# Second cast buffer, weight tiles in halves, kv copy on VectorE, output transposes in psB

## Chip, cores, metric

The kernel runs on all 8 cores of one Trainium2 chip, each with one of the 8 batch rows of `x` ([4096, 2048] float32) and a full copy of the five weight matrices ([2048, 2048] float32). No core talks to another. The metric is the device time of the slowest core in microseconds (us).

## What is computed

A LayerNorm, a causal linear attention with an ELU+1 feature map, and a gate from a projection with ternary weights:

```python
xn = (x - mean) / sqrt(var + 1e-5)
q, k, v = xn @ Wq + bq, xn @ Wk + bk, xn @ Wv + bv      # 16 heads of 128
qf, kf = elu(q) + 1, elu(k) + 1
# chunks of 128 rows; kv_ex, ksum_ex: sums over the chunks before
A = where(causal, qf @ kf.T, 0)
out = (qf @ kv_ex + A @ v) / (qf @ ksum_ex + A.sum(-1) + 1e-6)
s = out @ Wo + bo
scale = mean(abs(W));  Wt = clip(round(W / scale), -1, 1)
y = x + s * silu(layernorm(xn) @ Wt)
```

## The kernel before

The 4096 rows are worked through in 8 superchunks of 512 rows (`for sc in range(nsc)`, L464), each of four chunks of 128 rows. Activations are kept transposed (features on partitions) in bf16: `xnT`, `xn2T` (normalized twice, the input of the ternary projection), `qat`, `kfT`, `vg`, each [128, 16 x 512].

A superchunk is this sequence on TensorE:

- `emit_ln_B` (L421): for each of the four chunks j, 16 transposes of `xns` into the upper half of psB (L431) and 16 of `kftok` or `vtok` (used here for the normalized rows) into the lower half (L437). VectorE copies the lower half to `xnT` (L447), ScalarE scales the upper half to `xn2T` in 16 operations (L455). ScalarE makes the rows of chunks 2 and 3 in `emit_apply` (L409, L414) after the transposes of chunks 0 and 1.
- `proj_phase` (L469) for q, k and v: 16 output tiles each. A tile waits for its weight tile (128 x 2048 bf16, 512 KB) in the ring `wring` and for its bank of psA, and is 16 matmuls of 128 x 512 (L487). ScalarE (L502, L505) and VectorE (L511) take q and k out of psA, ScalarE alone v (L531).
- Attention, four chunks (L540): transposes of kfT and vg into psB (L546, L553), copied to `kftok` by VectorE (L560) and `vtok` by ScalarE (L565); scores into psA (L575), masked to `a_m` (L583, L589); inter plus intra products into psB (L603, L609); the normalizer into psA (L616, L622), its Ln and Exp on ScalarE (L629, L634); the chunk's kv product into psA (L641); VectorE multiplies into `qat` (L649) and adds psA to the float32 state `kvstate` (L657). ScalarE copies the state to bf16 `kvbf` (L669), VectorE adds and copies `ksumst` to `ksumbf` (L663, L666).
- `emit_ln_A` (L330) issues the next superchunk's statistics: VectorE sums (L349), ScalarE squares (L344), a chain of tiny operations, and the applies of chunks 0 and 1 (L389, L394). It is queued ahead of the evacuation of f.
- `proj_phase` for f (evacuated by ScalarE as Silu, L684) and o (L708, L716).
- Output, four chunks (L724): 16 transposes each (L733), VectorE adds them to the residual rows in `xres` (L741), POOL writes `y` (L750) and loads the residual of chunk j+2 (L320) into the same one of two buffers.

The first superchunk also converts the weights. `mk_step_convert` (L196) makes one step per 128 rows of a matrix: SP loads 1 MB into `xres[sl]`, sl = r % 2 (L203); VectorE casts to bf16 into `pcast[sl]` (L219); POOL writes it to the scratch tensor `wsc` in DRAM in two DMAs of 256 KB (L241). For f a first pass takes absolute sums (L209), then after `mk_step_scale` a second pass makes ternary values with three VectorE operations (L223, L226, L230). 16 steps each for q, k, v, o, f sums, one scale step, and 16 ternary steps stand in this order in `pro_steps`. `pump(2)` emits two of them after each chunk of `emit_ln_B` (L461) and after each output tile (L494); `stream_wtile` (L295) first pumps until the matrix it needs is complete. So two conversion steps stand between two weight loads on SP's queue, and two casts behind each tile's evacuation on VectorE's, until tile 8 of the first v phase.

Both entries of `pcast` are the same buffer, and a cast waits for the last write of either kind:

```python
        pcast = [pcast0, pcast0]                       # L142
                for cr in cast_rel:                    # L215
                    if cr is not None:
                        wait("vector", cr[0], cr[1])
```

Each engine runs its own list of instructions in the order in which the Python code emits them; semaphores hold them together. `psA_bank_rel[bk]` is what must have read a bank of psA before TensorE writes it again, `set_rel`/`wait_rel` the same for other buffers.

## Time and profile before

| | us |
|---|---|
| median of 2 runs | 4101.69 (4101.14 to 4102.23) |
| the profiled execution | 4104.62 |
| its span on the slowest core, from the first to the last instruction | 4103.1 |
| spans of the 8 cores | 4083.9 to 4103.1 |
| mean granted TensorE clock of the cores | 0.837 to 0.854 of full |
| TensorE busy with matmuls | 2820.6 (69%) |
| ScalarE busy | 1219.5 (30%) |
| VectorE busy | 973.9 (24%) |
| bytes moved | 581.66 MB, mean 142 GB/s |

The profile is of one execution on the slowest core. An engine's busy time is an average over stages with different limits, so it must be read by stage: the conversion, which lies within the first superchunk, and the seven superchunks after it. "DVE" is VectorE, "ACT" ScalarE, "PE" TensorE, "POOL" GpSimd, "SP" the queue that issues weight loads. "a <- b" in an idle time means that the engine stood before the instruction until b was done.

### The profile page before, as it was taken

The numbers are of one execution on the slowest core, as the hardware profiler recorded it, in microseconds if no ns is written. First come the engines' busy times: TensorE is split into PE (matmuls) and PEld (weight loads), VectorE is DVE, ScalarE is ACT, GpSimd is POOL, SyncE is SP. The second block draws the span as 40 slices with busy tenths as digits, with TensorE's granted clock in tenths as the row PEclk, the third lists the DMA queues.
The fourth block names the chain that finished last, engine by engine and source line by source line (L and its number), as shares of the span: only waits on it lengthen the run. The fifth ranks groups of instructions, "written<-read, shape, count | busy, mean of one in ns | idle before, by whom it ended". The sixth has DMA issues, their size and how long they took to land.

```text
span 4103.1 us, 41611 instructions; the slowest of 8 cores (4083.9 to 4103.1 us)
## 1 busy us (share of the span) xinstructions
PE 2820.6 (69%) x15876; PEld 1457.6 (36%) x15876; DVE 973.9 (24%) x957; ACT 1219.5 (30%) x1712; POOL 196.5 (5%) x268
## 2 busy tenths in 40 slices
PE   1033324346969696969696969786978598769976
PEld 1011111114434443444344434433444344434443
DVE  2111114324112412240223122212132212221221
ACT  4000001005143424342433343334333342424231
POOL 1111110110000000000000000000000000000000
PEclk9966667667989897989798979997998799889988
DMA  5566667452454145414541454235423543243323
GB/s 160 180 196 196 196 193 248 153 171 99 149 189 150 41 144 185 153 45 137 180 153 52 131 183 153 67 118 184 151 82 103 185 144 103 78 169 123 124 74 127
DMA packets 133056, 581.66 MB, mean 142 GB/s; under 512 B 16000, under 2 KB 16096, under 8 KB 108288
## 3 DMA queue, kind: packets, MB, share of 16 engines
q1 hardware_dynamic: 105984, 436.25, 32.8%
q0 software_dynamic: 26880, 142.74, 10.1%
q8 instruction: 134, 2.20, 0.2%
q14 instruction: 58, 0.48, 0.0%
HBM read 503.43 MB, written 75.50 MB: 141 GB/s over the span
## 4 chain that ended last, share of the span: by engine, by line
PE 58%; DMA 16%; ACT 9%; DVE 8%; issue 6%; POOL 2%; DVEq 0%; ACTq 0%; SPq 0%; POOLq 0%
PE psA L487 49%; DMA wsc<-pcast 12%; ACT xn2T L455 3%; DVE pcast L219 2%; POOL wsc L241 2%; ACT scr L629 2%; ACT scr L634 1%; DMA xres<-x 1%; DVE qat L649 1%; PE psB L431 1%; PE psB L546 1%; PE psB L553 1%; DMA y<-xres 1%; DMA wring<-wsc 1%; DVE a_m L583 1%
## 5 line engine op out<-in xcount | busy, mean ns | idle before, releaser
L487 PE MATMUL psA<-xnT,wring 128*128 128x512 bf16 x6144 | 1426.3, 397 | 589.9 <-DMA wring<-wsc 579.1
L487 PEld LDWEIGHTS psA<-xnT,wring 128*128 128x128 bf16 x6144 | 619.8, 101 | 1393.8 <-issue 733.1
L487 PE MATMUL psA<-xn2T,wring 128*128 128x512 bf16 x2048 | 484.0, 402 | 94.6 <-ACT vg L684 49.1
L487 PE MATMUL psA<-qat,wring 128*128 128x512 bf16 x2048 | 443.3, 379 | 0.0
L487 PEld LDWEIGHTS psA<-xn2T,wring 128*128 128x128 bf16 x2048 | 208.9, 103 | 367.1 <-issue 151.3
L487 PEld LDWEIGHTS psA<-qat,wring 128*128 128x128 bf16 x2048 | 200.4, 98 | 241.6
L716 DVE TENSOR_TENSOR xnT<-scr,vg 128x512 bf16<-128x512 f32 x128 | 88.6, 692 | 806.7 <-ACT scr L708 806.7
L502 ACT ACTIVATE scr<-psA,bs_q 128x512 f32<-128x512 f32 x128 | 88.0, 687 | 579.4 <-PE psA L487 572.9
L531 ACT ACTIVATE vg<-psA,bs_v 128x512 bf16<-128x512 f32 x128 | 88.0, 687 | 509.0 <-PE psA L487 509.0
L502 ACT ACTIVATE scr<-psA,bs_k 128x512 f32<-128x512 f32 x128 | 88.0, 687 | 473.6 <-PE psA L487 473.6
L431 PE MATMUL psB<-identb_s,xns 128*128 128x128 bf16 x512 | 59.5, 310 | 234.0 <-ACT xn2T L455 188.8
L708 ACT ACTIVATE scr<-psA,bs_o 128x512 f32<-128x512 f32 x128 | 88.0, 688 | 355.5 <-PE psA L487 355.5
L455 ACT ACTIVATE xn2T<-psB,lnb_sb,lnw_sb 128x128 bf16<-128x128 bf16 x512 | 182.2, 492 | 36.4 <-PE psB L431 36.4
L219 DVE CAST pcast<-xres 128x2048 bf16<-128x2048 f32 x64 | 78.5, 1227 | 476.5 <-DMA wsc<-pcast 476.5
L241 POOL DMA_DIRECT2D wsc<-pcast x160 | 141.1, 886 | 766.6 <-DVE pcast L219 515.1
L511 DVE SCALAR_TENSOR_TENSOR qat<-scr 128x512 bf16<-128x512 f32 x128 | 88.5, 692 | 350.1 <-ACT scr L505 350.1
L511 DVE SCALAR_TENSOR_TENSOR kfT<-scr 128x512 bf16<-128x512 f32 x128 | 88.5, 692 | 342.5 <-ACT scr L505 342.5
L684 ACT ACTIVATE vg<-psA 128x512 bf16<-128x512 f32 x128 | 74.2, 598 | 297.4 <-PE psA L487 297.3
L750 POOL DMA_DIRECT2D y<-xres x32 | 17.2, 537 | 2942.6 <-DVE xres L741 2896.3
L733 PE MATMUL psA<-identb_s,xnT 128*128 128x128 bf16 x512 | 63.7, 253 | 118.3 <-DVE xres L741 110.4
L431 PEld LDWEIGHTS psB<-identb_s,xns 128*128 128x128 bf16 x512 | 52.0, 144 | 240.2 <-issue 240.2
L649 DVE TENSOR_TENSOR qat<-psB,scr 128x2048 bf16<-128x2048 f32 x32 | 73.3, 2292 | 229.3 <-ACT scr L634 229.3
(97 smaller groups left out, 2209.3 us busy)
## 6 DMA issues: line engine op xcount, KB each, us to landing
wring<-wsc SPq DMA_DIRECT2D x640, 512.0 KB, 3.3
wsc<-pcast POOLq DMA_DIRECT2D x160, 256.0 KB, 6.0
xln<-x POOLq DMA_DIRECT2D x32, 1024.0 KB, 10.9
xres<-w_f SPq DMA_DIRECT2D x32, 1024.0 KB, 5.8
xres<-x POOLq DMA_DIRECT2D x32, 1024.0 KB, 7.4
y<-xres POOLq DMA_DIRECT2D x32, 1024.0 KB, 8.1
xres<-w_q SPq DMA_DIRECT2D x16, 1024.0 KB, 5.7
xres<-w_k SPq DMA_DIRECT2D x16, 1024.0 KB, 5.7
```

The lines of the kernel that those rows point to most:

```text
L219: op("vector", lambda e, sl=sl, cs=cslot: e.tensor_copy(cs[:, :], xres[sl][:, :]), [(s_dv, 1)])
L241: return e.dma_start(out=dst.transpose([1, 0, 2]), in_=s2)
L431: op("tensor", lambda e, t=t, xm=xnstm: e.transpose(psBT[:, 2048 + t * 128:2048 + (t + 1) * 128], xm[:, t * 128:(t + 1) * 128], identb[:, ...
L455: op("scalar", lambda e, t=t, j=j: e.activation(xn2T[:, t * T + j * 128: t * T + (j + 1) * 128], psBT[:, 2048 + t * 128:2048 + (t + 1) * 128],
L487: op("tensor", lambda e, k=k, ti=ti, bk=bk, rb=rhs_buf: e.matmul(psA[:, bk * 512:(bk + 1) * 512], wring[k % 6][:, ti * 128:(ti + 1) * 128] ...
L502: op("scalar", lambda e, bk=bk, to=to, esl=esl: e.activation(scr[:, esl[0]:esl[1]], psA[:, bk * 512:(bk + 1) * 512], AF.Exp, bias=biases[b ...
L511: e.scalar_tensor_tensor(dst[:, to * T:(to + 1) * T], scr[:, esl[0]:esl[1]], 1.0, scr[:, rsl[0]:rsl[1]], ALU.min, ALU.add), [(s_dv, 1)])
L531: op("scalar", lambda e, to=to, bk=bk: e.activation(vg[:, to * T:(to + 1) * T], psA[:, bk * 512:(bk + 1) * 512], AF.Identity, bias=biases[ ...
L629: op("scalar", lambda e: e.activation(scr[:, SQ_DUMP[0]:SQ_DUMP[1]], psA[:, :], AF.Ln, bias=epscol_f[:, :]), [(s_ac, 1)])
L649: op("vector", lambda e, j=j: e.tensor_tensor(bass.AP(qat, j * 128, [[NT * T, 128], [T, H], [1, 128]]), psB[:, :].rearrange("p (t c) -> p ...
L708: op("scalar", lambda e, to=to, bk=bk, ssl=ssl: e.activation(scr[:, ssl[0]:ssl[1]], psA[:, bk * 512:(bk + 1) * 512], AF.Identity, bias=bia ...
L716: op("vector", lambda e, to=to, ssl=ssl: e.tensor_tensor(xnT[:, to * T:(to + 1) * T], scr[:, ssl[0]:ssl[1]], vg[:, to * T:(to + 1) * T], A ...
```

## The change

Four parts:

1. `pcast` becomes two buffers, and a cast waits only for the write of the step that used the same one.
2. The weight ring has 10 slots of half a tile (128 x 1024 bf16, 256 KB) where it had 6 of a whole one. `stream_whalf` issues two DMAs per tile; TensorE waits for the first half ahead of the tile and for the second before its ninth matmul, which also gives the first half's slot free.
3. In attention VectorE makes `kvbf` directly (`kvstate` + psA, bf16) before it updates `kvstate`, and `ksumbf` likewise; ScalarE's copy of the state is gone. psA is given free, as before, by the update of `kvstate`. In the next chunk TensorE waits for VectorE's `kvbf`.
4. The output transposes go to the lower half of psB and no longer to banks 0 and 1 of psA; the output add reads psB and gives psB free.

```diff
-        NRING = 6
-        wring = [e_(nc.sbuf_tensor(f"wring{i}", [128, D], CDT)) for i in range(NRING)]
+        NRING = 10
+        wring = [e_(nc.sbuf_tensor(f"wring{i}", [128, D // 2], CDT)) for i in range(NRING)]
...
-        pcast0 = e_(nc.sbuf_tensor("pcast0", [128, D], CDT))
-        pcast = [pcast0, pcast0]
+        pcast = [e_(nc.sbuf_tensor(f"pcast{i}", [128, D], CDT)) for i in range(2)]
...
-                for cr in cast_rel:
-                    if cr is not None:
-                        wait("vector", cr[0], cr[1])
+                cr = cast_rel[sl]
+                if cr is not None:
+                    wait("vector", cr[0], cr[1])
...
-        def stream_wtile(m, to):
+        def stream_whalf(m, to, half):
             k = wtile_ctr[0]
             wtile_ctr[0] += 1
-            if k >= 6:
-                wait("sync", s_wfree, k - 5)
-            if to == 0:
+            if k >= NRING:
+                wait("sync", s_wfree, k - (NRING - 1))
+            if to == 0 and half == 0:
                 pump_until(PRO_READY[m])
                 wait("sync", s_sm[(m, 0)], s_sm[(m, 0)].n)
                 wait("sync", s_sm[(m, 1)], s_sm[(m, 1)].n)
...
-                in_=wsc[MIDX[m], to, :, :, :]), [(s_w[k % 6], 16)])
+                in_=wsc[MIDX[m], to, :, half * 8:(half + 1) * 8, :]),
+               [(s_w[k % NRING], 16)])
...
                 for to in range(NT):
-                    k, wn = stream_wtile(m, to)
+                    kA, wnA = stream_whalf(m, to, 0)
+                    kB, wnB = stream_whalf(m, to, 1)
                     bk = to % 4
-                    wait("tensor", wn[0], wn[1])
...
+                    wait("tensor", wnA[0], wnA[1])
                     for ti in range(NT):
+                        k = kA if ti < 8 else kB
...
+                        if ti == 8:
+                            incs = [(s_wfree, 1)]
+                            wait("tensor", wnB[0], wnB[1])
...
-                wait("vector", s_ac, ac_kvbf)
+                op("vector", lambda e: e.tensor_tensor(
+                    kvbf[:, :], kvstate[:, :], psA[:, :], ALU.add), [(s_dv, 1)])
+                dv_kvbf = s_dv.n
+                wait("vector", s_dv, dv_ksum4)
+                op("vector", lambda e, j=j: e.tensor_tensor(
+                    ksumbf[:, :], ksumst[:, :],
+                    kscur[:, j * H:(j + 1) * H], ALU.add), [(s_dv, 1)])
+                dv_ksbf = s_dv.n
                 op("vector", lambda e: e.tensor_tensor(
                     kvstate[:, :], kvstate[:, :], psA[:, :], ALU.add), [(s_dv, 1)])
                 dv_kvupd = s_dv.n
...
-                op("vector", lambda e: e.tensor_copy(
-                    ksumbf[:, :], ksumst[:, :]), [(s_dv, 1)])
-                wait("scalar", s_dv, dv_kvupd)
-                op("scalar", lambda e: e.copy(kvbf[:, :], kvstate[:, :]),
-                   [(s_ac, 1)])
-                ac_kvbf = s_ac.n
+                dv_kvbf_state[0] = dv_kvbf
...
-                for bk in range(2):
-                    r0 = psA_bank_rel[bk]
-                    if r0 is not None:
-                        wait("tensor", r0[0], r0[1])
+                wait_rel("tensor", "psB")
...
-                        psAT[:, t * 128:(t + 1) * 128],
+                        psBT[:, t * 128:(t + 1) * 128],
...
-                    psAT[:, 0:2048].rearrange("p (t c) -> p t c", c=128),
+                    psBT_lo3d(),
...
-                psA_bank_rel[0] = (s_dv, dv_out)
-                psA_bank_rel[1] = (s_dv, dv_out)
+                set_rel("psB", (s_dv, dv_out))
```

VectorE in the first superchunk, between two attention chunks, before (L649 multiplies into `qat`, L560 is the next chunk's copy of `kftok`; in brackets the semaphores waited for):

```order
L649 TENSOR_TENSOR qat<-psB,scr 128x16x128 [waits pe,ac]
L657 TENSOR_TENSOR kvstate<-kvstate,psA 128x2048 [waits pe,ac]
L663 TENSOR_TENSOR ksumst<-ksumst,kscur 128x16 [waits dv]
L666 CAST ksumbf<-ksumst 128x16 [waits dv]
L560 COPY kftok<-psB 128x2048 [waits pe]
L583 TENSOR_TENSOR a_m<-psA,maskb_s 128x1024 [waits pe]
```

and the same place after (lines of the changed kernel):

```order
L654 TENSOR_TENSOR qat<-psB,scr 128x16x128 [waits pe,ac]
L661 TENSOR_TENSOR kvbf<-kvstate,psA 128x2048 [waits pe]
L665 TENSOR_TENSOR ksumbf<-ksumst,kscur 128x16 [waits dv]
L669 TENSOR_TENSOR kvstate<-kvstate,psA 128x2048
L675 TENSOR_TENSOR ksumst<-ksumst,kscur 128x16 [waits dv]
L565 COPY kftok<-psB 128x2048 [waits dv,pe]
L588 TENSOR_TENSOR a_m<-psA,maskb_s 128x1024 [waits pe]
```

A second addition over 128 x 2048 stands ahead of the update of `kvstate` and of the copy of `kftok`.

VectorE in the first q phase, conversion steps behind a tile's evacuation, before (`st_k0` and `st_k1` are the semaphores of the scratch writes of even and odd steps, `xl0` and `xl1` those of the loads):

```order
L511 SCALAR_TENSOR_TENSOR qat<-scr 128x512 [waits ac]
L219 CAST pcast0<-xres0 128x2048 [waits xl0,st_k0,st_k1]
L219 CAST pcast0<-xres1 128x2048 [waits xl1,st_k0,st_k1]
L511 SCALAR_TENSOR_TENSOR qat<-scr 128x512 [waits ac]
L219 CAST pcast0<-xres0 128x2048 [waits xl0,st_k0,st_k1]
```

and after:

```order
L516 SCALAR_TENSOR_TENSOR qat<-scr 128x512 [waits ac]
L217 CAST pcast0<-xres0 128x2048 [waits xl0,st_v0]
L217 CAST pcast1<-xres1 128x2048 [waits xl1,st_v1]
L516 SCALAR_TENSOR_TENSOR qat<-scr 128x512 [waits ac]
L217 CAST pcast0<-xres0 128x2048 [waits xl0,st_v0]
```

The order is the same; each cast waits for one of the two scratch semaphores.

TensorE at the end of a superchunk, before (L733 the output transposes of all four chunks, L431 and L437 the next LayerNorm's first):

```order
L733 MATMUL psA<-identb_s,xnT 128x128 [waits ac,dv]
L733 MATMUL psA<-identb_s,xnT 128x128 [waits dv] x63
L431 MATMUL psB<-identb_s,xns 128x128 [waits ac,ini,dv]
L431 MATMUL psB<-identb_s,xns 128x128 x15
L437 MATMUL psB<-identb_s,kftok 128x128 x16
```

and after:

```order
L737 MATMUL psB<-identb_s,xnT 128x128 [waits dv,ac]
L737 MATMUL psB<-identb_s,xnT 128x128 [waits dv] x63
L431 MATMUL psB<-identb_s,xns 128x128 [waits ac,ini,dv]
L431 MATMUL psB<-identb_s,xns 128x128 x15
L437 MATMUL psB<-identb_s,kftok 128x128 x16
```

The order is unchanged; both now write psB, and L431's wait for `dv` means the last output add where it meant the last chunk of attention.

## Rows read from the trace of the kernel before

**Rows 1.** The page, part 4: chain that ended last, by line.

```profile
PE psA L487 49%; DMA wsc<-pcast 12%; ACT xn2T L455 3%; DVE pcast L219 2%; POOL wsc L241 2%; ACT scr L629 2%; ACT scr L634 1%; DMA xres<-x 1%; DVE qat L649 1%; PE psB L431 1%; PE psB L546 1%; PE psB L553 1%; DMA y<-xres 1%; DMA wring<-wsc 1%; DVE a_m L583 1%
```

**Rows 2.** Waits: engine, line, waited for: us in total, times, longest.

```profile
PE psA L487 <- DMA wring<-wsc: 579.1, 41, 106.6
...
DVE pcast L219 <- DMA wsc<-pcast: 476.5, 62, 10.4
```

**Rows 3.** Windows by stage: us, PE, PEld, DVE, ACT, POOL, clock, DMA share, GB/s.

```profile
41.00:175.00 134.00, 10.71 (x96) 10.00 (x96) 23.67 (x20) 30.14 (x68) 26.88 (x31) 1.00 0.55 169
190.00:470.00 280.00, 86.64 (x240) 30.18 (x240) 46.43 (x46) 20.04 (x32) 52.86 (x60) 0.64 0.62 196
...
640.00:710.00 70.00, 35.55 (x112) 12.84 (x112) 33.32 (x20) 8.87 (x14) 0.00 (x0) 0.74 0.75 267
726.00:885.00 159.00, 43.78 (x117) 15.01 (x116) 49.67 (x41) 4.81 (x7) 22.91 (x26) 0.59 0.48 152
...
1180.00:1345.00 165.00, 165.00 (x766) 74.83 (x765) 31.02 (x36) 54.89 (x88) 0.00 (x0) 1.00 0.46 153
```

**Rows 4.** The casts of L219 from 190 to 640, and POOL's issues behind one.

```profile
L219 DVE CAST pcast<-xres x48: 1222/1227/1229, 191.8 to 632.6; 128x2048 bf16<-128x2048 f32 x48
...
455.68 1.76 POOL L241 DMA_DIRECT2D wsc<-pcast  x2 [8.42 <-DVE pcast L219]
```

**Rows 5.** Timeline, stage of absolute sums: start, us, engine, line, [idle before].

```profile
674.70 0.67 SPq L304 DMA_DIRECT2D wring<-wsc  x1
...
682.86 5.25 PE L487 MATMUL psA<-xnT,wring 128*128 128x512 bf16 x16 [5.93 <-DMA wring<-wsc]
```

**Rows 6.** Timeline, first casts and last round of the first transposes.

```profile
41.56 1.22 DVE L219 CAST pcast<-xres 128x2048 bf16<-128x2048 f32 x1
...
75.84 1.91 PE L437 MATMUL psB<-identb_s,vtok 128*128 128x128 bf16 x16
...
172.83 1.23 DVE L219 CAST pcast<-xres 128x2048 bf16<-128x2048 f32 x1 [5.25 <-DMA wsc<-pcast]
```

**Rows 7.** Timeline, first and fourteenth ternary step, and TensorE's restart.

```profile
726.37 1.29 DVE L223 TENSOR_SCALAR pcast<-xres,rscale 128x2048 bf16<-128x2048 f32 x1 [0.38 <-DVE rscale L268]
...
883.53 1.29 DVE L223 TENSOR_SCALAR pcast<-xres,rscale 128x2048 bf16<-128x2048 f32 x1 [8.96 <-DMA wsc<-pcast]
...
897.13 26.34 PE L487 MATMUL psA<-xnT,wring 128*128 128x512 bf16 x112 [8.38 <-DMA wring<-wsc]
```

**Rows 8.** Timeline, second superchunk's attention, between two chunks.

```profile
1378.33 2.28 DVE L657 TENSOR_TENSOR kvstate<-kvstate,psA 128x2048 f32<-128x2048 f32 x1
...
1380.97 1.23 DVE L560 COPY kftok<-psB 128x2048 bf16<-128x2048 bf16 x1
1382.25 1.19 PE L575 MATMUL psA<-qat,kfT 128*128 128x128 bf16 x16
...
1383.61 1.23 DVE L583 TENSOR_TENSOR a_m<-psA,maskb_s 128x1024 bf16<-128x1024 f32 x1 [1.42 <-PE psA L575]
```

**Rows 9.** Timeline, after the last chunk: the next LayerNorm and f.

```profile
1414.93 8.87 DVE L349 TENSOR_REDUCE lst<-xln 128x1 f32<-128x2048 f32 x4
...
1424.92 0.16 DVE L359 SCALAR_TENSOR_TENSOR lst<-lst 128x4 f32<-128x4 f32 x1 [0.58 <-ACT scr L344]
...
1438.42 21.87 PE L487 MATMUL psA<-xn2T,wring 128*128 128x512 bf16 x88 [7.02 <-ACT vg L684]
```

**Rows 10.** Timeline, boundary between the second and the third superchunk.

```profile
1559.81 1.86 PE L431 MATMUL psB<-identb_s,xns 128*128 128x128 bf16 x16 [0.21 <-issue]
...
1563.48 2.09 ACT L409 ACTIVATE kftok<-xln,lst 128x2048 bf16<-128x2048 f32 x1 [24.65 <-PE psB L437]
1565.14 2.29 DVE L741 TENSOR_TENSOR xres<-psA,xres 128x2048 f32<-128x2048 bf16 x1 [8.11 <-DMA xres<-x]
```

**Rows 11.** The page, part 6: DMA issues, KB each, us to landing.

```profile
wring<-wsc SPq DMA_DIRECT2D x640, 512.0 KB, 3.3
...
xres<-w_k SPq DMA_DIRECT2D x16, 1024.0 KB, 5.7
```

More of the change, by code:

```diff
@@ L51, in build_nc @@
     prog = {k: [] for k in ("sync", "gpsimd", "scalar", "vector", "tensor")}
-    s_w = [Sem(f"w{i}") for i in range(6)]
+    s_w = [Sem(f"w{i}") for i in range(10)]
     s_xl = [Sem(f"xl{i}") for i in range(2)]
@@ L147, in build_nc @@
         psBT = psB.ap().bitcast(BF16)
-        psAT = psA.ap().bitcast(BF16)
         for s in all_sems:
@@ L303, in stream_wtile @@
                 wait("sync", s_sm[(m, 1)], s_sm[(m, 1)].n)
-            op("sync", lambda e, m=m, to=to, k=k: e.dma_start(
-                out=wring[k % 6][:, :].rearrange("p (t d) -> p t d", d=128),
-                in_=wsc[MIDX[m], to, :, :, :]), [(s_w[k % 6], 16)])
-            return k, (s_w[k % 6], s_w[k % 6].n)
+            op("sync", lambda e, m=m, to=to, k=k, half=half: e.dma_start(
+                out=wring[k % NRING][:, :].rearrange("p (t d) -> p t d", d=128),
+                in_=wsc[MIDX[m], to, :, half * 8:(half + 1) * 8, :]),
+               [(s_w[k % NRING], 16)])
+            return k, (s_w[k % NRING], s_w[k % NRING].n)
         def load_xln(c):
@@ L325, in build_nc @@
         ac_kvbf = 0
+        dv_kvbf_state = [0]
         xres_handover = [False]
@@ L488, in proj_phase @@
                             psA[:, bk * 512:(bk + 1) * 512],
-                            wring[k % 6][:, ti * 128:(ti + 1) * 128],
+                            wring[k % NRING][:, (ti % 8) * 128:(ti % 8 + 1) * 128],
                             rb[:, ti * T:(ti + 1) * T],
@@ L596, in build_nc @@
                 wait("tensor", s_dv, dv_kftok)
-                wait("tensor", s_ac, ac_kvbf)
+                wait("tensor", s_dv, dv_kvbf_state[0])
                 for h in range(H):
@@ L661, in build_nc @@
                     psA_bank_rel[bk] = (s_dv, dv_kvupd)
-                wait("vector", s_dv, dv_ksum4)
+                wait("vector", s_dv, dv_ksbf)
                 vtiny(lambda e, j=j: e.tensor_tensor(
```

## Prediction

> **What bounds the kernel now.** I read the chain of waits first [rows 1]: TensorE's projection matmuls (L487) are 49% of it, and the DMA that writes converted weights to scratch (`wsc<-pcast`) is 12%. Then the list of waits [rows 2]: VectorE stood 476.5 us in front of the weight cast for that DMA, and TensorE 579.1 us for weight tiles (`wring<-wsc`). The windows by stage [rows 3] (columns: window, length, PE, PEld, DVE, ACT, POOL busy, granted clock, DMA share, GB/s) put all of it in the first superchunk: from 190 to 470 us PE is busy 31% of the time at a mean clock of 0.64 of full, while in the steady q, k and v phases (1180 to 1345) it is busy without a gap at clock 1.00, with the DMA engines at a share of 0.46. So there are two kernels: a conversion stage to about 897 us, bound by one chain (cast, write to scratch, next cast), and seven superchunks of about 420 us (from L431 at 1559.8 [rows 10] there are six of them, and the output's tail, to the end at 4103.1), bound by TensorE with stalls at attention, at the start of f and between superchunks. The change takes the chain of the first apart, and adds to the stalls of the second.
>
> **Conversion: two cast buffers.** A cast now waits for the write of the step before it; after, for that of the step two before.
>
> q, k and v weights of the later steps and o: 48 casts start from 191.8 to 632.6 us [rows 4], so one step takes (632.6 - 191.8)/47 = 9.38 us: cast 1.2, the handover and two POOL issues of 0.88 each (1.76 for two), the landing. With two buffers that whole cycle covers two steps, so 4.7 us a step is the floor of this loop. The next limit is the DMA engines. Two steps and one weight tile are 18.76 us and carry 196 GB/s x 18.76 = 3.68 MB; at the share of 0.62 that is 11.6 us of engine time, 5.8 us a step. In the stage of absolute sums (640 to 710) the engines carry 267 GB/s at 0.75, or 356 at a full share: 10.3 us, 5.2 a step. A third loop goes over two tiles: qat/kfT on DVE, two casts, the weight load, 16 matmuls, ACT. Its load took 8.2 us behind two 1 MB loads (issue at 674.70, PE at 682.86) [rows 5], then PE 5.3, ACT an estimated 1.5, DVE 3: 18 us per four steps, not binding. Bounds per step are thus 5.2 (nothing but bandwidth) and 9.4 (no gain). I take 6.0, a little above the engine time at 0.62, since landings lengthen as the queues fill: 47 x (9.38 - 6.0) = 159 us less, all on the path, since TensorE waits for it.
>
> The first 16 casts: from 41.6 to 172.8 us, 8.75 us each. The first eight are interleaved with the first LayerNorm's four rounds of transposes and copies, which ACT paces; the last round ends at 77.8 [rows 6], so the eighth cast comes at about 78. The last eight carry no weight tile: engine time 0.55 x 8.75 = 4.8 us a step (the window from 41) [rows 3], and I take 5.2, 42 us in all: the last at 120 and not 172.8, 53 us less.
>
> Ternary steps: DVE does 3.8 us each (three operations), from 726.4 to 883.5 thirteen steps at 12.1 us [rows 7]; the tile that closes the stall (PE at 897.13) is queued on SP behind the load that waits for this one. Two buffers allow 6.05 a step, the engine time 0.48 x 24.2/2 = 5.8. I take 6.5: 13 x 5.6 = 73 us less. Bounds 6.05 to 12.1.
>
> Absolute sums write nothing to scratch and keep their 20.5 us per two tiles: 0, perhaps 1 us less per tile, since PE starts on half a tile.
>
> Sum of the first stage: 53 + 159 + 73 = 285 us less (with all low bounds 330, with 8.0 a step throughout about 160).
>
> **The kv state (attention).** Before, DVE adds psA into kvstate at 1378.33 (2.28 us), which frees psA; ACT makes the bf16 copy beside it; DVE copies kftok at 1380.97; the scores (L575) start at 1382.25, held by PE's own transposes, and the mask follows at 1383.61, 1.36 later [rows 8]. After, DVE does the bf16 sum into kvbf first, then ksumbf, and only then the kvstate add that frees psA: 1378.33 + 2.2 + 0.17 + 2.28 = 1382.98, plus 0.25 of semaphore: L575 at 1383.2, about 1.0 us late. kftok is ready by then (1380.97 + 2.2 + 1.23 = 1384.4, just before the mask at 1384.6). The new op is not in the trace; its nearest row is the same add into f32, 2.28 us. If bf16 output ran twice as fast the delay would be 0; the other end is 2.4 (all of it in series). I take 1.0, three times per superchunk, 24 in all: 24 us. The copy taken from ACT (1.9 us) gives nothing here: what the next matmuls wait for is the mask, not ACT's vtok.
>
> After the last chunk f's first tiles start 2.4 us later but then stop anyway for ACT, which is in the next LayerNorm [rows 9]: PE resumes at 1438.42. In that LayerNorm DVE's four sums (8.87 us from 1414.93) begin 2.3 us later and ACT's squares 0.7 later, so the variance (L359, 1424.92, held by ACT) becomes DVE's and comes 1.8 later. Seven times 1.8, and once 2.4 at the end: 15 us. Here ACT's freed 1.9 us stops counting, since DVE is late next.
>
> **Output transposes into psB.** Before, they share psA banks 0 and 1 with nobody who waits. After, they share psB with the next LayerNorm's transposes (L431), which wait for both its parts. In [rows 10] L431 starts at 1559.81, beside the wait for the last residual load; the last output add runs 1565.14 to 1567.43, and after an add PE starts some 0.3 us later (in rows 8 the mask follows its matmuls as closely). After, L431 waits until 1567.7: 7.9 us. Behind it queue L437, ACT's applies (1563.48), ACT's 16 scalings and the whole ACT-bound stage up to q's first matmul, so nothing absorbs it. The other boundaries have the same two loads in front; I take 7.8 x 7 = 55 us. The gain is nothing: the first output transposes never waited for a psA bank, and q's banks are free long before q starts. This term is the surest.
>
> **Weight halves.** Twice the DMAs, five tiles of room instead of six, and a wait amid each 16 matmuls. In the steady phases PE never waits for weights; 766 matmuls in 165 us are 3.45 us per tile of 16 [rows 3], against 3.41 for 16 x 512 columns at 2.4 GHz, so all that a tile boundary with its waits now costs is 0.04 us: 0 taken for another wait, at most 0.04 x 640 = 26 us. The Trainium skill (DMA: Bandwidth & Descriptors, Measured) speaks against this part: batch transfers to 1 MiB, since each pays a fixed part. By it 512 KB take about 3.2 us, and the trace has that (3.3 from issue to landing [rows 11]); halves would take about 2.6.
>
> Sum: -285 + 24 + 15 + 55 = -191. Against the profiled execution's 4104.6 that is 3913.6; the median of the runs shown, 4101.7, is 2.9 lower: 3911, which I round to 3910, 4.7% less.
>
> **The rivals.**
> 1. VectorE's casts block POOL's issues. Until now no cast could run while POOL issued a write to scratch, since each waited for the writes; with two buffers they meet. If each cast held POOL, or was held, for its full 1.23 us, a step would cost 7.2, not 6.0: 47 x 1.2 + 13 x 1.2 + 8 x 1.2 = 82 us back, 3992. For it: the casts' speed (2048 elements in 1.23 us, against 2.28 for an f32 add). Against: POOL is busy only 1.8 of 6 us a step. The Trainium skill (SBUF — State Buffer, the shared port pair) says that a cast in a 2-port mode locks GpSimd out of the port with which it writes descriptors. The trace of before has no overlap to test it. Chance 0.12.
> 2. The DMA side gives out sooner: 8 cores at once, landings that grow with the load, 8.0 us a step. Then the gains are 47 x 1.38 = 65, 13 x 4.1 = 53 and, with 6.9 a step in the first part, 40: 158 less, 94 more, 4038. Against: 267 GB/s at 640 to 710, in the same stage on all cores. Chance 0.07.
> 3. Slower: the landing of the scratch writes stretches in proportion, so that two in flight take as long as one after the other. Its place is `wsc<-pcast`, its price the whole 285 us, and the 94 us of steady additions stand: 4196, 2.3% slower. It decides from a step of 9.0 us on, where 47 x 0.4 + 13 x 3.1 + 35 is the 94 again. Against: the write's engine time is small beside its landing, and 0.38 of the engines' time is free [rows 3]. Chance 0.03. Another one on this side: if two halves don't overlap and each needs over 1.73 us of the steady 3.45 per tile, PE stalls; at a whole tile's 3.3 us each, by 3.1 us a tile, far slower. Against: in the stage at 640 to 710 several transfers of one queue are clearly in flight. Chance 0.02.
> 4. The change isn't effective in conversion because another wait stands right behind (the weight load into `xres`, still two buffers). It lands in 5.7 us [rows 11] against 12 us of cycle per buffer, so it stays inside the 6.0 a step of the forecast.
>
> **How the numbers follow.** The forecast's mechanism has 0.76; 0.12, 0.07 and 0.05 as above. Its own range: all low bounds (-330, and 15 less of attention) 3850; 6.8 us a step 3965. With rival 1 inside, and a little beyond the low bound, the range is 3845 to 3995. Faster by over 2% (below 4020, about what a measurement here can tell from no change): 0.76 + 0.12, less 0.01; within 2% 0.08; slower 0.05.
>
> **What would show it.** Right: casts about 6 us apart between 140 and 420, the DMA share there over 0.9, the wait of casts for `wsc` down from 476 to under 300 us; q's first matmul near 130, the free run of v before 620 (897 now); superchunks 420 + 7.8 + 4.7 = about 432 us long; L431's wait for the last output add, 7.8 x 7; `L575` waiting about 0.8 for DVE; no PE wait for `wring` after the first superchunk. Wrong: POOL's issue longer than 0.89 us (rival 1), casts near 8 us apart (rival 2), superchunks of 420 (the psB term false), or any `wring` wait in q, k, v of the later ones.

## The result, and the profile after

The changed kernel takes 4009.5 us (median; the lowest run is 3991.3), the kernel before 4102.4 beside it on the same chip: a ratio of 0.977, with a 95% interval from 0.974 to 0.980. In some executions of every kernel here the cores of one die, or of both, show a lower granted clock and take longer; the medians are of all executions, the ratios of the others alone. It is faster by 2.3%, about 95 us, where 191 were forecast; 3910 was predicted, and the time lies above the range's end of 3995. The profiled execution took 3996.1 us with a span of 3994.5 on core 1; the spans of the eight cores run from 3961.7 to 3994.5. All positions of these two kernels below are of core 1, as before; each experiment is read on its own slowest core, where no other is named.

The page after, part 4, the chain that ended last by line (against [rows 1]):

```profile
PE psA L492 50%; DMA wsc<-pcast 6%; ACT xn2T L455 3%; DMA y<-xres 3%; DMA wring<-wsc 2%; DVE kvbf L661 2%; ACT scr L634 2%; ACT scr L639 2%; DMA xres<-x 1%; PE psB L431 1%; PE psB L608 1%; DVE lst L349 1%; PE psB L614 1%; POOL wsc L239 1%; PE psA L580 1%
```

The scratch writes fell from 12% of the chain to 6%. New in it are `kvbf` (L661) and three lines of attention on TensorE (L580, L608, L614). The list of waits after (engine, line, waited for: us in total, times, longest), against [rows 2]:

```profile
PE psA L492 <- DMA wring<-wsc: 337.9, 46, 65.9
...
ACT scr L634 <- PE psA L627: 218.3, 32, 8.1
...
DVE pcast L217 <- DMA wsc<-pcast: 152.2, 45, 10.1
...
PE psB L431 <- DVE xres L745: 56.9, 7, 8.9
...
PE psA L580 <- DVE ksumst L675: 21.7, 24, 1.0
```

TensorE's wait for weight tiles is 241 us shorter, VectorE's for the scratch writes 324 us. The last two are the forecast's new waits, of about the forecast size. (The profile names `ksumst` L675 in the last row; by the code L580 waits for the update of `kvstate`, L669, just before it.) The second row is not in the forecast at all: ScalarE waits 218.3 us for the last matmuls of attention's denominators, which in the kernel before was 149.2 (ACT L629 for PE L622, 32 times). TensorE hands over 69 us later in all, and its own wait for VectorE is only 21.7 of that.

The windows by stage (columns as in [rows 3]): the conversion in q, k and v, the ternary steps, a steady stretch of matmuls, one attention chunk.

```profile
125.00:450.00 325.00, 144.16 (x402) 50.09 (x403) 83.04 (x76) 31.72 (x50) 97.51 (x100) 0.70 0.91 288
...
541.00:630.00 89.00, 33.46 (x97) 11.78 (x96) 49.45 (x39) 4.83 (x7) 31.09 (x27) 0.71 0.78 260
950.00:1115.00 165.00, 163.98 (x760) 74.39 (x761) 31.78 (x37) 55.70 (x90) 0.00 (x0) 1.00 0.53 150
1151.00:1172.00 21.00, 12.21 (x128) 11.44 (x128) 10.90 (x9) 5.75 (x3) 0.00 (x0) 0.66 0.00 1
```

The conversion's DMA share rose from 0.62 to 0.91 and its rate from 196 to 288 GB/s. TensorE's steady stretch is as it was; the DMA share there is 0.53 for 0.46 at about the same rate, which costs nothing in it. The attention chunk's window has the same 128 matmuls as that of a chunk before, but in 21 us and not 17, and at a mean granted clock of 0.66. The same window of the kernel before:

```profile
1378.00:1395.00 17.00, 9.50 (x128) 8.92 (x128) 8.33 (x8) 7.64 (x4) 0.00 (x0) 0.80 0.00 1
```

### The conversion stage

The casts of L217 in q, k and v (against [rows 4]), and all issues of L239:

```profile
L217 DVE CAST pcast<-xres x48: 1219/1227/1680, 147.4 to 436.2; 128x2048 bf16<-128x2048 f32 x48
...
L239 POOL DMA_DIRECT2D wsc<-pcast x160: 885/885/1831, 41.7 to 644.8; - x160
```

(436.2 - 147.4)/47 = 6.14 us a step, forecast 6.0. The step was right; what was lost lies at the ends. The sixteenth cast comes at 129.4 instead of 172.8, 43 us earlier (forecast 53): the eighth comes at 80.1, nearly where the forecast had it, and the eight steps behind it take 6.2 us each and not 5.2. From the last of the 48 casts (before at 632.6) to the first ternary step the absolute sums take 99.7 instead of 93.8 us: 6 more (forecast 0); why is not shown. The thirteen ternary steps run from 535.9 to 625.0, 89 us for 157 (forecast 73 less, measured 68). And then something new, TensorE's restart and the first attention:

```profile
645.66 2.15 POOL L311 DMA_DIRECT2D xln<-x  x4
```

```profile
657.16 1.89 PE L492 MATMUL psA<-xnT,wring 128*128 128x512 bf16 x8 [1.45 <-DMA wring<-wsc]
662.03 2.30 PE L492 MATMUL psA<-xnT,wring 128*128 128x512 bf16 x7 [2.98 <-DMA wring<-wsc]
```

As soon as POOL has issued the last scratch write it issues six loads of 1 MB of the next inputs (four for `xln`, two for `xres`), and beside these 6 MB TensorE stops for single halves, five times. From the fourteenth ternary step to the first attention it takes 65 instead of 53 us, 11 more. The six loads alone don't do that. The kernel with two cast buffers and whole tiles (e1, below) issues them as well, and its last 112 matmuls run in one piece:

```profile
655.39 24.33 PE L486 MATMUL psA<-xnT,wring 128*128 128x512 bf16 x112 [2.98 <-DMA wring<-wsc]
```

Over the eight cores the stretch from the fourteenth ternary step to the first attention takes 52 to 56 us in e1 (mean 53.5), 52 to 68 in the changed kernel (60.2) and 53 to 67 in e4, which has the halves and is otherwise e1 (61.0). In sum attention begins 247 us earlier on this core (936.9 to 689.5); forecast 285.

### The steady stage

Attention, VectorE's and TensorE's rows between two chunks (against [rows 8]):

```profile
1149.85 2.29 DVE L654 TENSOR_TENSOR qat<-psB,scr 128x2048 bf16<-128x2048 f32 x1 [8.55 <-ACT scr L639]
1152.06 2.28 DVE L661 TENSOR_TENSOR kvbf<-kvstate,psA 128x2048 bf16<-128x2048 f32 x1
...
1154.34 2.28 DVE L669 TENSOR_TENSOR kvstate<-kvstate,psA 128x2048 f32<-128x2048 f32 x1
...
1159.13 1.23 DVE L588 TENSOR_TENSOR a_m<-psA,maskb_s 128x1024 bf16<-128x1024 f32 x1 [0.95 <-PE psA L580]
...
1170.39 2.29 DVE L654 TENSOR_TENSOR qat<-psB,scr 128x2048 bf16<-128x2048 f32 x1 [8.90 <-ACT scr L639]
```

```profile
1157.09 1.86 PE L580 MATMUL psA<-qat,kfT 128*128 128x128 bf16 x16 [0.90 <-DVE ksumst L675]
...
1160.56 0.31 PE L614 MATMUL psB<-a_m,vtok 128*128 128x128 bf16 x1
1160.66 0.31 PE L608 MATMUL psB<-qat,kvbf 128*128 128x128 bf16 x1
...
1164.61 0.26 PE L627 MATMUL psA<-a_m,onescol_b 128*128 128x128 bf16 x1
1164.71 0.22 PE L621 MATMUL psA<-qat,ksumbf 128*128 128x128 bf16 x1
1164.77 0.22 PE L627 MATMUL psA<-a_m,onescol_b 128*128 128x128 bf16 x1
```

The same place on TensorE in the kernel before (L575, in [rows 8], stands behind L553):

```profile
1378.89 1.87 PE L546 MATMUL psB<-identb_s,kfT 128*128 128x128 bf16 x16 [3.67 <-DVE qat L649]
1380.55 1.91 PE L553 MATMUL psB<-identb_s,vg 128*128 128x128 bf16 x16
...
1385.04 0.22 PE L609 MATMUL psB<-a_m,vtok 128*128 128x128 bf16 x1
1385.09 0.22 PE L603 MATMUL psB<-qat,kvbf 128*128 128x128 bf16 x1
```

L580 begins 1.1 us later behind L661 than L575 did behind L657 (5.03 for 3.92), as forecast. But its 16 matmuls take 1.86 instead of 1.19 us, and then the matmuls of L608 and L614 start 0.107 us apart, until 1164.61; from there on 0.055 apart. All of them started 0.055 apart in the kernel before. The two distances are the lower and the upper level of TensorE's clock (1.2 and 2.4 GHz). Before, the engine went without a gap through its two rounds of transposes (L546, L553, at the lower level) into L575, and the clock rose there. After, it stands for 0.90 us in front of L580, and the clock rises only 7.5 us after L580's start. From 1160.56 to 1164.61 there are 38 distances at 0.107 instead of 0.055: 2.0 us. The chunk takes 20.54 us, for 17.00 (L649 at 1376.12 and 1393.12): 1.1 of waiting, 0.7 in L580, and 1.7 from the mask to the last denominator.

Over the eight superchunks of this core the three distances between L654s add up to 481.0 us, for 412.3 before: 68.7 more, 2.9 a chunk. Forecast 24.

Not every chunk has this form. In 23 of these 24, between 29 and 40 of the 64 matmuls from L608 to L627 run at the lower level (none of them in the kernel before). But in seven of the 24 L580 itself is at the upper level, in spite of its stand, and in six of those the clock falls again behind it:

```profile
1137.72 1.05 PE L580 MATMUL psA<-qat,kfT 128*128 128x128 bf16 x16 [0.99 <-DVE ksumst L675]
...
1140.76 0.27 PE L608 MATMUL psB<-qat,kvbf 128*128 128x128 bf16 x1
```

From 1140.76 the matmuls start 0.107 us apart, until 1144.13.

The next LayerNorm (against [rows 9]) and a boundary between superchunks (against [rows 10]):

```profile
1193.11 2.28 DVE L661 TENSOR_TENSOR kvbf<-kvstate,psA 128x2048 bf16<-128x2048 f32 x1
...
1207.50 0.16 DVE L359 SCALAR_TENSOR_TENSOR lst<-lst 128x4 f32<-128x4 f32 x1 [0.17 <-DVE lst L356]
...
1221.41 3.15 PE L492 MATMUL psA<-xn2T,wring 128*128 128x512 bf16 x7 [7.34 <-ACT vg L691]
```

```profile
1347.91 2.29 DVE L745 TENSOR_TENSOR xres<-psB,xres 128x2048 f32<-128x2048 bf16 x1 [7.28 <-DMA xres<-x]
...
1350.35 1.86 PE L431 MATMUL psB<-identb_s,xns 128*128 128x128 bf16 x16 [7.25 <-DVE xres L745]
```

The variance (L359) now follows VectorE's own sums and not ScalarE, and TensorE resumes f 28.3 us after L661 where it was 26.1 after L657: 2.2 a superchunk (forecast 1.8). L431 waits 7.25 us here for the last output add, 56.9 in all over seven boundaries, 8.1 each (forecast 7.8).

So on core 1: 247 less, then 69 in attention, 18 in LayerNorm and f, 57 at the boundaries more; that gives -103, and the spans differ by 4103.1 - 3994.5 = 108.6. The two gaps against the forecast are 38 us at conversion and 45 us at attention.

### The profile page after: what moved, and what is told of

It is laid out like the page before. It is cut to its first block, busy times and chain, and to the rows that moved or that the text cites. A ratio compares the mean times of both kernels' runs of the same rounds, so it can differ in the third digit from the quotient of the medians.

```text
span 3994.5 us, 43386 instructions; the slowest of 8 cores (3961.7 to 3994.5 us)
## 1 busy us (share of the span) xinstructions
PE 2860.2 (72%) x15876; PEld 1499.8 (38%) x15876; DVE 1049.1 (26%) x989; ACT 1161.7 (29%) x1680; POOL 218.7 (5%) x268
## 4 chain that ended last, share of the span: by engine, by line
PE 58%; DMA 14%; ACT 9%; DVE 8%; issue 8%; POOL 1%; DVEq 0%; SPq 0%; ACTq 0%; POOLq 0%
PE psA L492 50%; DMA wsc<-pcast 6%; ACT xn2T L455 3%; DMA y<-xres 3%; DMA wring<-wsc 2%; DVE kvbf L661 2%; ACT scr L634 2%; ACT scr L639 2%; DMA xres<-x 1%; PE psB L431 1%; PE psB L608 1%; DVE lst L349 1%; PE psB L614 1%; POOL wsc L239 1%; PE psA L580 1%
## 5 line engine op out<-in xcount | busy, mean ns | idle before, releaser
L431 PE MATMUL psB<-identb_s,xns 128*128 128x128 bf16 x512 | 59.6, 309 | 285.2 <-ACT xn2T L455 193.1
L239 POOL DMA_DIRECT2D wsc<-pcast x160 | 163.2, 1024 | 474.4 <-DVE pcast L217 264.3
L431 PEld LDWEIGHTS psB<-identb_s,xns 128*128 128x128 bf16 x512 | 52.0, 142 | 291.6 <-issue 291.6
L737 PE MATMUL psB<-identb_s,xnT 128*128 128x128 bf16 x512 | 63.9, 253 | 118.5 <-DVE xres L745 110.4
L565 DVE COPY kftok<-psB 128x2048 bf16<-128x2048 bf16 x32 | 39.2, 1225 | 364.5 <-PE psB L551 358.4
```

The costliest lines, as they stand in the source:

```text
L239: return e.dma_start(out=dst.transpose([1, 0, 2]), in_=s2)
L431: op("tensor", lambda e, t=t, xm=xnstm: e.transpose(psBT[:, 2048 + t * 128:2048 + (t + 1) * 128], xm[:, t * 128:(t + 1) * 128], identb[:, ...
```

## The experiments

Ratios are to the kernel before, run on the same chip; the interval is at 95%. Three edits recur: the kv part and the psB part (output transposes) taken back to the kernel before, word for word, and the second cast buffer alone.

**One part at a time.** e1 is the kernel before with two cast buffers, and five whole weight slots where it had six, so that they fit:

```diff
-        NRING = 6
+        NRING = 5
...
-        pcast0 = e_(nc.sbuf_tensor("pcast0", [128, D], CDT))
-        pcast = [pcast0, pcast0]
+        pcast = [e_(nc.sbuf_tensor(f"pcast{i}", [128, D], CDT)) for i in range(2)]
...
-                for cr in cast_rel:
-                    if cr is not None:
-                        wait("vector", cr[0], cr[1])
+                cr = cast_rel[sl]
+                if cr is not None:
+                    wait("vector", cr[0], cr[1])
```

> The kernel before with the second cast buffer alone (the ring has 5 whole tiles instead of 6, for room). Theory: the conversion gain is all this part's, TensorE restarts in v about 250 us earlier (near 645, before 897), and the superchunks keep their 419.6 us: about 4100 - 250 = 3850 us. Rival, the halves feed TensorE sooner in the conversion: whole tiles cost 5 us per tile pair there, the gain is some 50 us smaller, 3900.

Measured: 0.943 (0.936 to 0.950), 3870.5 in the profiled execution. The 48 casts stand from 149.0 to 445.9, 6.3 us a step.

e2 is the changed kernel with the kv part taken back:

```diff
-                op("vector", lambda e: e.tensor_tensor(
-                    kvbf[:, :], kvstate[:, :], psA[:, :], ALU.add), [(s_dv, 1)])
...
+                wait("scalar", s_dv, dv_kvupd)
+                op("scalar", lambda e: e.copy(kvbf[:, :], kvstate[:, :]),
+                   [(s_ac, 1)])
```

> The changed kernel without the kv part. Theory (the clock of TensorE rises later because its scores matmuls wait 0.9 us for psA): attention chunks 1 to 3 go from 20.4 back to 17.0 us and f resumes 2.2 us sooner: 24 x 3.4 + 7 x 2.2 = 97 us less, 3900. Rival (only the 1.0 us of the longer VectorE chain, the rest has another cause): 24 + 15 = 39 us less, 3958.

Measured: 0.957 (0.955 to 0.959), against 0.977 for the changed kernel: the kv part costs 0.020, 82 us, nearer to the theory's 97 than to the rival's 39; the two intervals (0.002 and 0.003 either way) leave the 39 out. L608 and L614 are back at the upper level in every chunk (x512 each, over the whole run):

```profile
L614 PE MATMUL psB<-a_m,vtok 128*128 128x128 bf16 x512 | 63.8, 219 | 0.0
L608 PE MATMUL psB<-qat,kvbf 128*128 128x128 bf16 x512 | 63.8, 219 | 52.5 <-DVE a_m L588 50.6
```

The same groups in the changed kernel (busy us, mean ns):

```profile
L614 PE MATMUL psB<-a_m,vtok 128*128 128x128 bf16 x512 | 97.5, 284 | 0.0
L608 PE MATMUL psB<-qat,kvbf 128*128 128x128 bf16 x512 | 96.5, 282 | 50.2 <-DVE a_m L588 49.8
```

e3 takes back the psB part instead:

```diff
-                wait_rel("tensor", "psB")
+                for bk in range(2):
+                    r0 = psA_bank_rel[bk]
+                    if r0 is not None:
+                        wait("tensor", r0[0], r0[1])
...
-                        psBT[:, t * 128:(t + 1) * 128],
+                        psAT[:, t * 128:(t + 1) * 128],
```

> The changed kernel with the output transposes in psA again. Theory: L431 no longer waits for the last output add (8.1 us, 7 times): 57 us less, 3940. Rival, the time comes back in a wait for the residual loads or for ScalarE: 0 to 20 us less, 3980.

Measured: 0.962 (0.960 to 0.964): the psB part costs 0.015, 62 us (forecast 55), and the wait of the first LayerNorm transposes for `xres` is gone from the list.

e4 takes back both, so that what is left is e1 with half tiles for whole ones:

> The changed kernel with both kv and psB undone, so second cast buffer and weight halves. Theory: the parts add up, 97 + 57 less: 3843, and within 10 us of the cast buffer alone (halves worth nothing either way). Rival: halves cost in the conversion (more transfers on a full DMA): 20 us or more above the cast buffer alone; or they gain there, 20 or more below.

Measured: 0.946 (0.940 to 0.952). Beside e1's 0.943 the two intervals overlap nearly whole, so the ratio shows neither a gain nor a cost of the weight halves; one of 30 us would not show in it. The traces say a little more. In e4 the first attention comes at 701 us, in e1 at 687 (means of the eight cores). The stretch behind the fourteenth ternary step, above, has 7.5 us of that; the rest is no more than what kernels with the same conversion differ by (688 in the changed kernel, 700 in e2). From there to the end the eight cores need 3170 us in e4 and 3162 in e1 (means), and on the slowest core of each it is 3174.6 and 3175.8. In the steady stretch a tile costs what it did (760 matmuls in 165 us above). So the halves gained nothing and, in these traces, cost some 7 us at the restart. This answers to the rule weighed in the prediction, the Trainium skill's advice to batch transfers (DMA: Bandwidth & Descriptors, Measured): a half landed in 2.8 us (page after, part 6) where a whole tile took 3.3, so the fixed part is there to see, but it is hidden where TensorE has 3.45 us of work per tile. Only in the stretch after the ternary steps do stops for single halves show; the slowest core of e1 has two stops there, that of e4 five.

**Is it the stand of TensorE?** If a stand of under 1 us in front of the scores is what costs the clock, the kernel before must show the same with such a stand and nothing else. e5 puts a VectorE addition of 1600 columns (its result is not used) between the kvstate update and the copy of `kftok`, in the first three chunks, and lets the scores wait for it:

```diff
+                if j < NCH - 1:
+                    op("vector", lambda e: e.tensor_tensor(
+                        scr[:, 0:1600], kvstate[:, 0:1600], kvstate[:, 0:1600], ALU.add),
+                       [(s_dv, 1)])
+                    for bk in range(4):
+                        psA_bank_rel[bk] = (s_dv, s_dv.n)
```

> The kernel before, with one more VectorE operation (an add of 1600 columns into scratch space that nobody reads, 1.8 us) between ksumbf and kftok for chunks 0 to 2, which psA's release waits for: TensorE stands about 0.8 us before the scores matmuls, as in the changed kernel, but all its other work is as before. Theory (a stand of TensorE there delays the rise of its clock): the chunk takes 17.0 + 0.8 + 2.3 = 20.1 us, with the 64 matmuls of L603 to L622 at 0.11 us instead of 0.055 each for more than half of them; 24 x 3.1 = 74 us above before. Rival (no such effect, the changed kernel's extra comes from the bf16 sum itself or its buffers): 17.8 us, 24 x 0.8 = 19 us above.

Measured: 1.013 (1.010 to 1.015), 52 us: between the theory's 74 and the rival's 19. One chunk of e5, first VectorE, then TensorE:

```profile
1382.67 1.82 DVE L669 TENSOR_TENSOR scr<-kvstate 128x1600 f32<-128x1600 f32 x1
...
1386.98 1.22 DVE L583 TENSOR_TENSOR a_m<-psA,maskb_s 128x1024 bf16<-128x1024 f32 x1 [1.36 <-PE psA L575]
```

```profile
1384.95 1.86 PE L575 MATMUL psA<-qat,kfT 128*128 128x128 bf16 x16 [0.71 <-DVE scr L669]
1388.35 0.27 PE L603 MATMUL psB<-qat,kvbf 128*128 128x128 bf16 x1 [1.54 <-DVE a_m L583]
1388.41 0.31 PE L609 MATMUL psB<-a_m,vtok 128*128 128x128 bf16 x1
1388.52 0.31 PE L603 MATMUL psB<-qat,kvbf 128*128 128x128 bf16 x1
```

It is the changed kernel's picture: 0.71 us of standing, L575 in 1.86, then distances of 0.107. The chunk takes 20.25 us. The three distances of all superchunks add up to 467.2, for 412.3 before: 54.9 more, of which 24 x 0.71 = 17 is standing and the rest is clock. 18 of the 24 chunks have 30 to 43 of their 64 matmuls (L603 to L622) at the lower level and take 19.1 to 20.9 us; the other six have none and take 17.8 to 18.3, which is the standing alone. The second adds and ScalarE's copy, which differ between the kernels, are not needed for the effect.

e6 is the same with 1150 columns, a stand of some 0.3 us:

> The same with 1150 columns (1.35 us): TensorE stands 0.3 us. Theory, if any stand at all delays the clock: 17.3 + 2.3 = 19.6 us a chunk, 62 us above before. If the delay grows with the stand: about 18.2. Rival without a clock effect: 17.3, 7 us above.

Measured: 1.004 (1.001 to 1.008). Most chunks take 17.3 to 17.6 us, but four of 24 take 18.7 to 19.0, with L603 at a mean of 228 ns (269 in e5, 219 before). The shorter stand costs the clock less often: chunks with matmuls from L603 to L622 at the lower level are 0 of 24 without a stand, 4 behind one of some 0.3 us, 18 behind some 0.71, and 23 behind some 0.90 in the changed kernel. Each count is from one execution of one core.

e7 goes the other way. It is the changed kernel, where TensorE repeats eight of its transposes of `vg` in chunks 1 to 3 while it would stand:

```diff
+                for h in range(8 if j > 0 else 0):
+                    op("tensor", lambda e, h=h, j=j: e.transpose(
+                        psBT[:, 2048 + h * 128:2048 + (h + 1) * 128],
+                        vg[:, h * T + j * 128: h * T + (j + 1) * 128],
+                        identb[:, :]))
```

> The changed kernel with 8 repeated transposes ahead of those of vg in chunks 1 to 3, which write what the real ones write again: TensorE is busy in the 0.9 us in which it stood before the scores matmuls. They start no sooner. Theory: the clock rises before L608, the chunk falls from 20.4 to about 18.1 us, 24 x 2.3 = 55 us less than the changed kernel. Rival (the stand isn't the cause): 20.4 us or more, no gain.

Measured: 0.965 (0.962 to 0.969), 47 us faster than the changed kernel for doing more work (the two intervals leave some 19 us either way). In the chunk below the stand shrinks to 0.45 us, and L585 and all behind it are at the upper level:

```profile
1142.68 1.05 PE L585 MATMUL psA<-qat,kfT 128*128 128x128 bf16 x16 [0.45 <-DVE ksumst L680]
1145.28 0.22 PE L613 MATMUL psB<-qat,kvbf 128*128 128x128 bf16 x1 [1.55 <-DVE a_m L593]
```

The distances between chunks add up to 446.1, 35 less than in the changed kernel. The scores start no sooner, so that the 1.1 us of waiting stays in every chunk (26 of the 69 us); the 35 are most of the other 42. 17.97 us is the best chunk, and eight of 24 still have half of their short matmuls at the lower level and take 19.3 to 19.5. The eight transposes both fill the stand and give the engine work ahead of it; which of the two holds the clock is not told apart.

**Can the kv part be had without the stand?** e8 and e11 update kvstate first, which frees psA as early as before, and then copy it to bf16 on VectorE, SBUF to SBUF:

```diff
-                op("vector", lambda e: e.tensor_tensor(
-                    kvbf[:, :], kvstate[:, :], psA[:, :], ALU.add), [(s_dv, 1)])
-                dv_kvbf = s_dv.n
...
+                op("vector", lambda e: e.tensor_copy(
+                    kvbf[:, :], kvstate[:, :]), [(s_dv, 1)])
+                dv_kvbf_state[0] = s_dv.n
```

> The changed kernel with the kv part in another order on VectorE: kvstate is updated first and psA given free, then kvbf is copied from kvstate in SBUF (about 1.2 us), nothing on ScalarE. Theory: psA is free as early as before, TensorE doesn't stand before the scores, kftok comes 1.2 us later but still before the mask: 17.0 to 17.4 us a chunk, 75 us less than the changed kernel. Rival (any second pass on VectorE costs its own length): 18.2 us, 50 less.

e8 gave no ratio. The same kernel was run again, as e11:

> The same kernel as e8, whose comparison didn't come to a verdict. Its undisturbed cores had all 64 matmuls at 0.055 us each and chunks of 17.2 us. Theory: 24 x 3.3 us less than the changed kernel (0.9768 of before, about 4007), so 3925 to 3935, a ratio of 0.957 to 0.960, like the kernel without the kv part (0.9568). Rival, something else on VectorE grows by the extra pass: 0.965 or more.

Measured: 0.964 (0.953 to 0.974), its lowest run 3921.9. The interval is wide and takes in both theories, 0.957 to 0.960 and 0.965 or more; the trace decides. The chunk shown takes 17.27 us, and the copy costs 1.23 in place of a second add of 2.28:

```profile
1128.02 2.29 DVE L654 TENSOR_TENSOR qat<-psB,scr 128x2048 bf16<-128x2048 f32 x1 [7.16 <-ACT scr L639]
...
1132.78 1.23 DVE L675 CAST kvbf<-kvstate 128x2048 bf16<-128x2048 f32 x1
...
1145.29 2.29 DVE L654 TENSOR_TENSOR qat<-psB,scr 128x2048 bf16<-128x2048 f32 x1 [7.16 <-ACT scr L639]
```

L608 and L614 are at 219 ns on average again. Nothing stands in front of the scores, and the clock stays. Over all 24 distances the chunks take 411.1 us, for 412.3 in the kernel before: made in this order, the copy on VectorE has no price in attention that can be seen.

**What bounds a conversion step at 6.1?** e9 is e1 with the loads of the q, k, v and o weights halved; the second half of their columns is stale, so the kernel leaves out half of that input traffic and the output is not the reference's.

```diff
+                nc_ = 1024 if (mode == "cast" and not (m == "q" and r < 2)) else 2048
...
-                    out=xres[sl][:, :], in_=w_in[m][r * 128:(r + 1) * 128, :]),
+                    out=xres[sl][:, 0:nc_], in_=w_in[m][r * 128:(r + 1) * 128, 0:nc_]),
```

> The cast-buffer kernel (e1) with the conversion loads of q, k, v and o cut to half their columns (0.5 MB for 1 MB), so that wrong weights are made from the second half; casts and scratch writes keep their size. It tells what bounds a step, 6.4 us in the changed kernel. Theory, the DMA engines (share 0.91): 3.68 MB per two steps become 2.63 MB, a step falls to about 4.8 us, the floor of the scratch-write loop being 4.7. Rival, the scratch-write loop itself, stretched by POOL and VectorE blocking each other: 6.0 us or more a step.

One execution: 3816.6 us, casts from 139.6 to 405.0, 5.65 us a step. It fell between the two expectations. The windows of e9 and of e1 over the same stretch:

```profile
125.00:440.00 315.00, 150.34 (x437) 53.08 (x438) 90.55 (x81) 34.17 (x54) 97.99 (x97) 0.73 0.76 232
```

```profile
125.00:440.00 315.00, 136.96 (x384) 47.94 (x384) 75.84 (x72) 30.39 (x48) 91.08 (x98) 0.68 0.90 282
```

At a share of 0.76 a step of 5.65 us holds 4.3 us of engine time, so the engines alone don't set it. The step lost 0.7 of 6.3, and the scratch write still took 7.3 us to land (8.2 in e1). An estimate from these rows: cast 1.2, two issues 2.0 and the landing 7.3 are 10.5 us of the 11.3 that a buffer's two steps take in e9, and 1.2, 1.9 and 8.2 are 11.3 of 12.6 in e1. The step is thus mostly the write's own loop, and the load on the DMA engines comes in through the landing, 6.0 us in the kernel before. The forecast's floor of 4.7 for this loop kept the landing as it was. One execution bears this, and how much of the landing is load is not settled.

e10 is e1 with the casts on ScalarE, where they take 1.90 us, to see what VectorE's casts do to POOL:

```diff
-                    op("vector", lambda e, sl=sl, cs=cslot: e.tensor_copy(
-                        cs[:, :], xres[sl][:, :]), [(s_dv, 1)])
...
+                    op("scalar", lambda e, sl=sl, cs=cslot: e.copy(
+                        cs[:, :], xres[sl][:, :]), [(s_ac, 1)])
```

> The cast-buffer kernel (e1) with the casts of q, k, v and o on ScalarE (about 2.0 us each) instead of VectorE (1.2 us, in which POOL can't issue). Theory (VectorE's casts hold up POOL's issues): all 128 issues behind them take 0.89 us again, none 1.4 or 1.8; the step hardly moves, since the DMA engines bound it: 6.2 to 6.6 us, the whole within 10 us of e1. Rival (the blocking is what keeps a step above 6.0): 20 us or more below e1. Rival without any blocking by VectorE: the long issues stay.

Measured: 0.941 (0.937 to 0.945), beside e1's 0.943 (0.936 to 0.950): no difference. POOL's issues from 125 to 440, first of e10, then of e1 (busy us, mean ns):

```profile
L247 POOL DMA_DIRECT2D wsc<-pcast x100 | 88.3, 887 | 229.0 <-ACT pcast L223 211.1 <-issue 17.8
```

```profile
L240 POOL DMA_DIRECT2D wsc<-pcast x98 | 92.0, 943 | 228.3 <-DVE pcast L218 201.4 <-issue 26.3
```

So VectorE's casts do hold up POOL: 943 ns for an issue, and 887 without them. But the step stays at 6.1 us. The casts on ScalarE are 0.67 us longer than on VectorE, and stand in the same loop, so a gain of that size from the shorter issues could be hidden.

e1 and e10 beat both kernels: 3866 and 3854 in their lowest runs, 5.7 and 5.9% less than before.

## Why the prediction was wrong

Its direction and most of its mechanisms held; the gain was half of what it said. By its steps:

- **Step of 6.0 us in q, k and v: right.** 6.14, at a share of 0.91 as foretold, and 152 us less for 159.
- **The ends of the conversion: mis-sized.** "53 us less" for the first casts was 43 (its step of 5.2 was 6.2), "73" for the ternary steps 68, the absolute sums took 6 more for 0, and the restart of TensorE 11 more for 0. The last had no term: the prediction did not ask what POOL issues right behind the last scratch write, and how half tiles fare beside it. What lengthened the first casts and the absolute sums stays open. 247 less on core 1, not 285; over the eight cores the first attention comes on average 243 us earlier.
- **Attention: the step that failed.** "I take 1.0, three times per superchunk, 24 in all: 24 us." The 1.0 us was right for the start of the scores (1.1), and its cost was 2.9 us a chunk, 69 in all. The delay was taken as a delay of VectorE's chain, with no term for TensorE's clock. It is also a stand of TensorE ahead of 80 short matmuls, and in 23 of 24 chunks the granted clock then was at its lower level for about half of them: e5 makes 2.3 us a chunk in the kernel before by a stand of 0.71 alone, e7 takes 35 of the 69 us away by repeated transposes, and e2 and e11, which have no stand, have no such matmuls. The trace of before had what was needed: L546 and L553 at the lower level, and L575, without a gap behind them, where the clock rises.
- **LayerNorm and f: right**, 2.2 us for 1.8 a superchunk; that VectorE's sums become the late ones is in the row of L359.
- **psB: right**, 56.9 us of waiting for 55 forecast, and 62 by e3.
- **Halves: right** in the steady phases (e4 against e1). The term of 0 left out the restart after the ternary steps, where they cost some 7 us on the mean core, 11 on this one.

The two main errors of the sum go the same way: 38 us too much gain in the conversion and 45 too little cost in attention. Of its own signs the share over 0.9 came (0.91), casts 6 us apart (6.1) and the casts' wait under 300 us (152); superchunks of 432 us did not: from the second to the last they are 440 apart.

**The rivals.** Rival 1 (casts block POOL) is half true; its sign, an issue longer than 0.89 us, came, and the rule of the Trainium skill (SBUF — State Buffer, the shared port pair) agrees with the trace: the issues last 1024 ns on average and up to 1831 (886 before), single casts up to 1680 ns, and in the ternary part a pair of issues beside VectorE's work took 2.84 us, another 1.76:

```profile
540.21 2.84 POOL L239 DMA_DIRECT2D wsc<-pcast  x2 [100.42 <-DVE pcast L228]
```

But taking the casts off VectorE gains nothing (e10), and the full 1.2 us a step, and its 3992 us, did not come: the step was 6.14 and not 7.2. That the time lies near 3992 is chance: the missing microseconds are elsewhere. Rival 2 (8.0 us a step) and rival 3 (writes stretch until nothing is gained) fell: landings went from 6.0 to 8.1 us, not to 12. Rival 4, another wait right behind, did not show: the loads of q, k, v and o landed in 6.1 to 8.6 us, and no cast waits for one in the list.

## What to carry to other kernels

A wait that is added in front of a short burst of matmuls can cost more than its length, here 2.9 us for 1.1: read in the trace at which clock level the matmuls behind it run, and what the engine did without a gap to get there. A second buffer gains only up to the next limit, and the ends of the stage it speeds up (what is issued right behind it) want terms of their own. Where the end of one stage and the start of the next came to share a PSUM buffer, the whole wait counted at each boundary (8.1 us, seven times). A part of a change that only costs is best found by taking the parts back one at a time.

## What was unexpected of the hardware

- Behind a stand of 0.90 us in front of 16 matmuls TensorE was at its lower level for about half of the next 64 short matmuls in 23 of 24 chunks, and behind one of 0.71 in 18; without a stand, in the kernel before, e2 and e11, in none. In the chunk shown for the changed kernel that is 2.4 us, beside the 1.1 of waiting. Stands of some 0.3 us did it in four chunks of 24.
- The upper level, once reached, was not kept either: in six of those 23 chunks it was there in L580 and was lost again by the first matmuls of L608 and L614.
- The kernel with eight useless transposes in each of these chunks was 47 us faster than the one without (e7 against the changed kernel).
- With two cast buffers the DMA engines carried 288 GB/s at a share of 0.91 in a mix of 1 MB loads, scratch writes in short runs and weight tiles, where one buffer had them at 196; the eight cores lie at 282 to 293, at the same time.
